# Token selection in two groups, moved into the sequence stage and into the attention

## What is computed

```python
# layer 1: recurrent mixing of the sequence
xk, xv, xr = (x * mix + shifted(x) * (1 - mix) for each of k, v, r)
k, v, r = xk @ Wk.T, xv @ Wv.T, xr @ Wr.T
per step: out = (a + exp(u + k) * v) / (b + exp(u + k)); a = a * ew + exp(k) * v; b = b * ew + exp(k)
x = layernorm(x + (sigmoid(r) * out) @ Wo.T)
# layer 2: a transformer block on 63 of the 512 tokens of each sequence
weights = x @ router_w + router_b
thr = the 64th largest weight; sel_idx = places of the 63 largest, sorted
q, k, v = rope(rmsnorm(x_sel) @ wq), rope(rmsnorm(x_sel) @ wk), rmsnorm(x_sel) @ wv     # 16 heads
x1 = x_sel + softmax(q k^T / 4 + mask[sel_idx, sel_idx]) v @ wo
x2 = x1 + gelu(rmsnorm(x1) @ w1) @ w2
x = layernorm(scatter(x2 * weight) + x * (weight <= thr))
```

## Time and profile before

| | us |
|---|---|
| median of 3 runs | 900.95 (900.33 to 901.28) |
| the profiled execution, its own time | 907.34 |
| its span, first to last instruction | 905.6 |

### The profile page before, as it was taken

The page is one execution under the profiler, slowest core; times in us unless marked ns, Lnnn a source line. Parts: engine busy times, 40 slices in busy tenths (PEclk is TensorE's granted clock), DMA queues, the critical chain, the costliest instruction groups (busy, mean ns, idle before and its releaser), DMA issues. The chain is left out here.

```text
span 905.6 us, 12959 instructions
## 1 busy us (share of the span) xinstructions
PE 779.3 (86%) x4228; PEld 522.4 (58%) x4228; DVE 729.3 (81%) x1505; ACT 496.5 (55%) x825; POOL 437.3 (48%) x303
## 2 busy tenths in 40 slices
PE   7999999999999999999999607397788888799983
PEld 4455554545555554545455405395566666699983
DVE  4689999999999999999999788446777787347773
ACT  2566757676676767676676421063567676431210
POOL 1667686868677786868686505444100000001223
PEclk9999999999999999999999855598999999999996
DMA  7122222231322223221310122342000000000000
GB/s 203 35 82 82 93 82 93 73 100 58 96 78 81 93 81 93 81 93 59 103 58 29 42 70 58 105 117 93 1 2 1 0 1 2 2 1 13 23 24 35
DMA packets 37317, 55.14 MB, mean 61 GB/s; under 512 B 3360, under 2 KB 26528, under 8 KB 37280
## 3 DMA queue, kind: packets, MB, share of 16 engines
q1 hardware_dynamic: 34464, 46.28, 16.4%
q0 software_dynamic: 2816, 8.39, 3.1%
HBM read 35.78 MB, written 18.87 MB: 60 GB/s over the span
## 5 line engine op out<-in xcount | busy, mean ns | idle before, releaser
L623 PE MATMUL ps<-arena,wa 128*128 128x512 f32 x768 | 337.0, 595 | 6.0 <-DMA wa<-w_attn 4.3
L623 PEld LDWEIGHTS ps<-arena,wa 128*128 128x128 f32 x768 | 146.2, 191 | 178.4 <-issue 169.0
L547 POOL TENSOR_TENSOR arena<-arena 128x1024 f32<-128x1024 f32 x32 | 75.5, 2360 | 123.5 <-issue 70.2
L637 PE MATMUL ps<-wa,arena 128*128 128x256 f32 x512 | 133.3, 383 | 0.0
L531 POOL TENSOR_TENSOR arena<-arena 128x512 f32<-128x512 f32 x93 | 128.1, 1407 | 4.6 <-ACT arena L915 4.6
L599 POOL TENSOR_TENSOR fst<-fst,mhalf 128x2 f32<-128x2 f32 x8 | 5.8, 720 | 235.8 <-DVE fst L1448 235.8
L928 ACT ACTIVATE arena<-arena 128x256 f32<-128x256 f32 x128 | 66.3, 590 | 67.8 <-DVE arena L1183 67.8
L1129 DVE TENSOR_TENSOR_SCAN arena<-ewb,ps 128x511 f32<-128x511 f32 x64 | 74.5, 1205 | 27.6 <-ACT ps L886 27.5
L637 PEld LDWEIGHTS ps<-wa,arena 128*128 128x128 f32 x512 | 88.4, 193 | 6.8
L538 POOL TENSOR_TENSOR arena<-arena 128x1024 f32<-128x1024 f32 x32 | 75.1, 2348 | 7.1 <-ACT arena L902 7.1
L635 PE MATMUL ps<-ident,arena 128*128 128x128 f32 x256 | 51.0, 281 | 27.3 <-POOL arena L547 27.3
(11 more groups left out here) (179 smaller groups left out, 1431.7 us busy)
## 6 DMA issues: line engine op xcount, KB each, us to landing
arena<-x_chan SPq DMA_DIRECT2D x32, 512.0 KB, 3.5
out<-arena SPq DMA_DIRECT2D x32, 512.0 KB, 3.3
arena<-x_chan SPq DMA_DIRECT2D x64, 127.8 KB, 3.2
wa<-w_attn SPq DMA_DIRECT2D x1, 1024.0 KB, 7.9
arena<-w_up SPq DMA_DIRECT2D x1, 1024.0 KB, 4.8
arena<-w_down SPq DMA_DIRECT2D x1, 1024.0 KB, 5.6
wqk<-w_qk SPq DMA_DIRECT2D x1, 512.0 KB, 4.6
wv<-w_v SPq DMA_DIRECT2D x1, 256.0 KB, 5.3
```

Source lines behind the costliest of these rows:

```text
L547: g.tensor_tensor(gg[s.par][:, :, :], num[s.par][:, :, :], ld[s.par][:, :, :], ALU.mult).then_inc(g_ready, 1)
L623: last = mm(bank[:, o, :], wa[:, m, c, o * P:(o + 1) * P], rhs, start=(c == 0), stop=(c == CC - 1))
L637: last = mm(psY[:, j, :], gg[s.par][:, c, tokens], wa[:, 3, c, :], start=False, stop=(c == CC - 1))
```

## The change

The 32 sequences are selected in two groups: group A is the first 18 (pairs 0 to 8, `SA` = 18, `NA` = 9), group B the other 14.

- Group A's selection runs in the sequence stage. VectorE has a slice of it in each of periods 21 to 30, between the numerator and the statistics; the rounds have MAX8 and MATCH_REPLACE8 but no FIND_INDEX8. A token's slot is found by counting: a scan over the tokens that are above the 63rd value or tie with it (`slots_chosen`). TensorE turns the weights in period 22 and the slots in period 27, and picks values in 28 to 30, in a bank of the key or gate projections.
- Group B's selection runs in periods 0 to 7 of the attention, before and after the softmax (`selection_early`, `selection_late`).
- Values, token index, sine and cosine are all picked by the one-hot matmul (`picks`); the tables of sine and cosine are made once at the start of the launch. The root mean square of a token comes from the statistics.
- The masks are gathered, turned, copied and picked pair by pair inside the attention: four transposes and four accumulated matmuls more on TensorE in each period, a copy on VectorE (`mask_copy`), two small copies on ScalarE (`mask_keep`).
- GpSimd gathers rows and masks through the attention and takes over the scaling of the inputs, and the last additions of the rotation (`rope_end`). It clears the value tiles in period 31. The softmax's sums stay in PSUM. The weights of the MLP are split in eight pieces in periods 11 to 17, with ScalarE.
- In the sequence stage ScalarE's order is new: the reciprocal of n-1 stands ahead of the exponentials of n, `rows_of` is one sequence later and stands ahead of the gate's logarithm. The gate's exponential is written to PSUM, and the clamp reads it there. VectorE does the statistics of n-2 ahead of the shift of n-3. The loop covers periods 4 to 19, and all else, with the attention and the MLP, is written out.

The diff, cut to what the prediction speaks of:

```diff
...
+            def gather_rows(q, batch):
...
+                g.indirect_dma_start(xsel(q), None, out_rows[0:SA * T, :] if q < NA else out_rows,
+                                     bass.IndirectOffsetOnAxis(ap=row_i[:, q:q + 1], axis=0)).then_inc(rows_in[q % 8], 16)
...
+            def rope_end(q):
...
+                for half, op in ((0, ALU.subtract), (1, ALU.add)):
+                    last = g.tensor_tensor(dst[:, :, half, :], dst[:, :, half, :], tmp[:, :, half, :], op)
+                last.then_inc(rope_done, 1)
...
+            def value_tiles_cleared():
...
+                for k in range(RING):
+                    g.memset(vblk[k], 0.0).then_inc(zeros_made, 1)
+                pool.wait_ge(zeros_made, RING)
+                pool.wait_ge(which_half, 1)
...
                 if at.exists():
                     log_sum_of(at)
+                if not isinstance(at.n, int):
+                    return
+                if at.n == 29:
+                    for q in range(0, 3):
+                        gather_rows(q, 1)
+                if at.n == 30:
+                    gather_rows(3, 2)
+                if at.n == 31:
+                    value_tiles_cleared()
             periods(pool, period)
+            last_periods(period, past=B + 1)
+            pool.wait_ge(y_ready, B)
...
+            last_periods(period, B + 1, B + 2)
+            gather_mask(0)
+            gather_mask(1)
+            normed(1)
...
+            for q in range(NP + 4):
+                if 4 <= q:
+                    normed2(q - 4)
+                if q < NP:
+                    rope_end(q)
+                if q + 2 < NP:
+                    normed(q + 2)
+                    x_of(q + 2)
+                if q + 5 < NA:
+                    gather_rows(q + 5, 2 if q == 0 else 3)
+                if q == 6:
+                    for late in range(NA, NA + 3):
+                        gather_rows(late, 4)
+                if q == 7:
+                    for late in range(NA + 3, NP):
+                        gather_rows(late, 5)
+                if q + 3 < NP:
+                    gather_mask(q + 3)
...
+                for m, bank, ready, used in ((0, psK, k_ready, den_done), (1, psV, v_ready, num_done), (2, psR, r_ready, clamp_done)):
                     if s.had(1):
                         pe.wait_ge(used, s.n)
...
+            def picks(first, past, bank, col):
...
+                for n in range(first, past):
+                    at_v = col + (PICK + 32 * tables_of(first)) * (n - first)
+                    for j in range(TJ):
+                        last = mm(ps[:, bank, at_v:at_v + 16], oh[:, n, j, :], tok_halves[:, 2 * n:2 * n + 2, j, :], start=(j == 0), stop=(j == TJ - 1))
+                    for h in range(tables_of(first)):
+                        at_t, table = at_v + 16 + 32 * h, min(2 * n + h, MB - 1)
+                        for j in range(TJ):
+                            last = mm(ps[:, bank, at_t:at_t + 32], oh[:, n, j, :], trig_halves[:, table * TJ + j, :], start=(j == 0), stop=(j == TJ - 1))
+                last.then_inc(values_picked, 1)
...
+                if n == 22 or 27 <= n <= 30:
+                    pe.wait_ge(clamp_done, n + 1)
+                if n == 22:
+                    weights_turn(0, SA, False)
+                if n == 27:
+                    slots_turn(0, SA, 5, 0)
+                if 28 <= n <= 30:
+                    picks(3 * (n - 28), 3 * (n - 28) + 3, 4, 0)
...
+            def att_period(n):
+                at = pair(n)
+                if n + 1 < NP:
+                    hn_turn(pair(n + 1))
+                    mask_turn(pair(n + 1))
+                if n < NP:
                     project_qk(at)
-                if at.is_pair(2):
...
-                    scores(at.back(1))
-                if at.below(NP):
-                    qk_turn(at, at.n + 2 if at.back(-1).below(NP) else NP)
-                if at.is_pair(4):
-                    hn2_turn(at.back(4), at.n + 1 if at.below(NP) else NP)
...
-                if s.had(2):
-                    act.wait_ge(sum_done, s.n - 1)
-                a.activation(er[s.par][:, :, :], psR[:, :, :], ACT.Exp, scale=-1.0).then_inc(er_done, 1)
+                a.activation(psR[:, :, :], psR[:, :, :], ACT.Exp, scale=-1.0).then_inc(er_done, 1)
...
+                    reciprocal_of(at.back(1))
                 if at.exists():
                     exp_k_of(at)
-                if at.had(1) and at.back(1).exists():
-                    reciprocal_of(at.back(1))
                 if at.back(-1).exists():
                     differences_scaled(at.back(-1))
                 if at.exists():
                     exp_r_of(at)
                     ln_den_of(at)
+                if at.had(4) and at.back(4).exists():
+                    rows_of(at.back(4))
+                if at.exists():
                     ln_gate_of(at)
                 if at.had(1) and at.back(1).exists():
                     evacuation_of(at.back(1))
-                if at.had(3) and at.back(3).exists():
-                    rows_of(at.back(3))
...
+            def mask_keep(at):
+                act.wait_ge(mask_picked, at.n + 1)
+                for b in range(2):
+                    block = slice(b * K, (b + 1) * K)
+                    last = a.activation(mall[block, at.n, :], ps[block, 7, 384 + b * K:384 + (b + 1) * K], ACT.Copy)
+                last.then_inc(mall_done, 1)
...
-                v.tensor_scalar(er[s.par][:, :, :], er[s.par][:, :, :], 2.0 ** 62, None, ALU.min).then_inc(clamp_done, 1)
+                if s.had(2):
+                    dve.wait_ge(sum_done, s.n - 1)
+                v.tensor_scalar(er[s.par][:, :, :], psR[:, :, :], 2.0 ** 62, None, ALU.min).then_inc(clamp_done, 1)
...
+                if isinstance(at.n, int):
+                    selection(at.n)
+                if at.had(2) and at.back(2).exists():
+                    statistics_of(at.back(2))
                 if at.had(3) and at.back(3).exists():
                     shift_of(at.back(3))
-                if at.had(2) and at.back(2).exists():
-                    statistics_of(at.back(2))
...
+            def top_round(ns, n):
+                eight = slice(8 * n, 8 * n + 8)
+                before = wsrc if n == 0 else wseq[(n - 1) % 2]
+                link(v.max(topv[0:ns, eight], before[0:ns, :]))
+                if n < K // 8 - 1:
+                    link(v.match_replace(wseq[n % 2][0:ns, :], topv[0:ns, eight], before[0:ns, :], NEG))
...
+                rows = slice(0, ns)
+                last, one = topv[rows, KC - 1:KC], ones[rows, :].to_broadcast([ns, T])
+                e, c = wseq[0][rows, :], wseq[1][rows, :]
+                if part == 0:
+                    v.tensor_copy(thr_rows[rows, :], topv[rows, K - 1:K].to_broadcast([ns, K]))
+                    v.tensor_scalar(e, wsrc[rows, :], last, None, ALU.is_equal)
+                    link(v.tensor_scalar(ties[rows, 0:KC], topv[rows, 0:KC], last, None, ALU.is_equal))
+                    v.tensor_tensor_scan(c, one, e, 0.0, ALU.mult, ALU.add)
+                    link(v.reduce_sum(need[rows, :], ties[rows, 0:KC], AX.X))
+                    link(v.scalar_tensor_tensor(e, c, need[rows, 0:1], e, ALU.is_le, ALU.mult))
+                else:
+                    link(v.scalar_tensor_tensor(e, wsrc[rows, :], last, e, ALU.is_gt, ALU.add))
+                    link(v.tensor_tensor_scan(c, one, e, 0.0, ALU.mult, ALU.add))
+                    v.tensor_tensor(e, e, c, ALU.mult).then_inc(slots_ready, 1)
...
+            def one_hot(q):
+                b = 2 * (q if q < NA else q - NA)
+                v.tensor_tensor(oh[:, q, :, :].rearrange("p j (h k) -> p j h k", h=2),
+                                slot_of[:, :, b:b + 2].unsqueeze(3).to_broadcast([P, TJ, 2, K]),
+                                slot_no[:, :].unsqueeze(1).unsqueeze(1).to_broadcast([P, TJ, 2, K]), ALU.is_equal).then_inc(oh_made, 1)
...
+            def selection(n):
+                if n == 21:
+                    token_weights(0, SA)
...
+                    top_round(SA, 0)
+                if n == 23:
+                    token_halves(0, SA)
+                    top_round(SA, 1)
+                if n == 24:
+                    top_round(SA, 2)
+                    top_round(SA, 3)
+                if n == 25:
+                    top_round(SA, 4)
+                    top_round(SA, 5)
+                if n == 26:
+                    top_round(SA, 6)
+                    top_round(SA, 7)
+                    slots_chosen(SA, 0)
+                    slots_chosen(SA, 1)
+                if n == 27:
+                    slots_copied_of(SA, 5, 0)
+                if 28 <= n <= 30:
+                    keep_values(3 * (n - 28), 3 * (n - 28) + 3, 4, 0, n - 27)
+                if 27 <= n <= 29:
+                    for q in range(3 * (n - 27), 3 * (n - 27) + 3):
+                        one_hot(q)
...
```

(31 more changed lines are left out.)

817 lines of the change are left out of this document (445 added, 372 removed).

## The result

The changed kernel takes 952.22 us (median of 4 runs, 949.78 to 956.17) against 900.64 (4 runs on the same chip): a ratio of 1.058, with a 95% interval of 1.053 to 1.063. The forecast was 881. The profiled execution has 954.52 us, span 952.8; the kernel before had 907.34, span 905.6.

The account below looks back on a forecast made before the run. It took TensorE and VectorE as both tight in the sequence stage, and a selection chain as the stretch to attack: 907.34 - 82.6 + 0.7 + 10 + 27 + 25 = 887.4, less 6.4 gives 881; range 832 to 914.

Parts of the forecast that it names:

- The loop of the sequence stage: Sequence-stage periods 2 to 25: period 16.0 instead of 15.58, plus 10 us, bounds minus 17 and plus 29.
- start: Start of the launch: one more DMA ahead of the first inputs, angle tables hidden beside the wait for inputs; plus 0.7 us.
- Rival one: Sequence stage: the gate's new place makes VectorE the bound through GpSimd; period 16.8, 915 us in all; chance 0.24.
- Rival two: Sequence stage: the sums slip through and TensorE sets the loop at 14.86; 835 us in all; chance 0.22.
- Group A's selection: Selection work placed in the sequence stage's late periods: plus 27 us, bounds 17 and 42.
- The gap: From last numerator to the attention's first projection: 107.6 us shrinks to 25 (20 to 35), minus 82.6.
- The attention: Fifteen attention periods at 10.55 plus 11 for group B, 169 against 144.7: plus 25 us, bounds 7 and 43.
- Rival three: Attention: GpSimd's queue delays it; period 11.6 instead of 10.55, 897 us, up to 915 with late gathers; chance 0.12.
- The tail: The drain and the 114 us of MLP keep their instructions: zero change.
- the distance between two scans: Sign in the sequence loop: 16.0 for the forecast, 14.9 for rival two, 16.8 for rival one.
- the sums above 1: Sign in the sequence loop: router sums averaging above 1 us would show rival one, 0.41 rival two.
- The dip of a few us in the clock: Sign between the stages: TensorE's clock at the upper level, or a dip of a few us.

Follow-up runs that it names:

- e3: Kernel before the change, with ScalarE taking the reciprocal ahead of the two exponentials of k: 898.63 us, ratio 0.982 to the kernel before.
- e8: Kernel before, with ScalarE's reciprocal ahead of the exponentials and its output rows between the two logarithms, four periods late: 926.86 us, ratio 1.028.
- e5: Changed kernel, with VectorE's shift again ahead of the statistics and ScalarE's output rows at the period's end, reciprocal still early: 876.98 us, ratio 0.971 to the kernel before.
- e6: Changed kernel, orders kept, each router sum a plain row sum with one SBUF input instead of two (other tokens chosen): 887.89 us, ratio 0.985 to the kernel before.
- e1: Changed kernel, with ScalarE again taking the reciprocal behind the two exponentials of k: 900.0 us, ratio 0.985 to the kernel before.
- e9: From e5, the two closing additions of the rotation moved from GpSimd back to VectorE: 884.64 us, ratio 0.970 to the kernel before.
- e11: From e5, group B's angle tables picked with one matmul in place of four a pair (angles wrong): 878.75 us, ratio 0.964 to the kernel before.
- e2: Changed kernel, with VectorE again taking the shift ahead of the statistics: 943.5 us, ratio 1.032 to the kernel before.
- e4: Changed kernel, with VectorE's statistics moved from the period's end to just behind the denominators: 920.49 us, ratio 1.008 to the kernel before.

## Why the prediction was wrong, step by step

**The loop of the sequence stage: the step that failed.** The forecast's parts were: VectorE's own work 13.0, waits of 3.0 taken with 3.8 as the upper bound, a period of 16.0. Own work measures 17.86 less 4.9, 13.0 exactly. The waits measure 4.9, outside the bound. It had the difference (0.6; 0.65 measured), the gate (2.35; 2.16) and one mix for the shift (0.9; 1.08), and left out the variance step, L1178 of before, which goes SBUF to SBUF like the clamp whose long time it had read, and which now stands against the first mix: 1.00. The taken value then leaned to a middle although for each kind of step in it a row spoke for the full price. And it was charged on 24 periods; the longer period lasts through the stage, in the ten selection periods too. The first 21 periods measure 41.6 more and the ten behind them 22 without the selection, 64 in place of the 10.7 for start and loop: 53 of the 57 us, and the selection is the rest.

**The cause given for it was half of it.** The prediction said that the reciprocal's new place moves the gate onto the sums. e3 shows that this move alone shortens the period, to 15.05. It needs the move of the rows as well (e8: 16.55), which the prediction doesn't mention: it costed ScalarE's reciprocal and passed over the other entry of the same queue that had moved. "GpSimd's work is moved" was argued from the exponentials behind the reciprocal; what decided was the 2.08 us of rows ahead of it.

One row of the prediction was misread: the clamp of 0.69 at 503.53 doesn't have GpSimd idle beside it but the power L554, which runs from 502.12 to 504.26. So even before, a row said that not every GpSimd instruction holds VectorE up.

**Rival one** had the mechanism and VectorE as the bound, and was priced at 915 with the same 16.8. With 2.28 more in thirty periods, 68 in place of its 29, its sum would have been 954. That this is near the 952 is partly luck: its 42 for the selection is 11 more than measured, and makes up for what gap, attention and tail cost beyond their terms. Rival two's TensorE-bound period of 14.86 exists as well: e5, e6 and e1's first part have 14.6 to 14.7. The Trainium skill, "SBUF — State Buffer", section "SBUF: two separate sides", was named for it, and by its rule the sum was this rival's; in the loop the trace agrees with the rule, down to the whole instruction being waited out (the second sum, begun 0.05 behind a gate of 2.35, ends 0.28 behind it), and the forecast should have followed it.

**Group A's selection: 27, measured 31.** Right within its bounds, though not by its terms. Periods 21 to 25 were held nearly free; in e5, where VectorE isn't bound by the waits, each of these five takes 17.4 to 18.2 against 14.7, 15 in all. In the kernel after they cost 5; that the work displaces some of the waits is a reading, not tested. The upper clock that the picks were priced at wasn't held (0.81 from 504 to 593). And of the 26.0 of the period that begins with scan 29, 7.4 are one wait that no term has. The prediction put the three row gathers at 4 or nothing. Behind them a sum waits not for one GpSimd instruction but for five:

```profile
563.66 0.94 POOL L565 DMA_INDIRECT kept<-out,row_i  x1 [0.30 <-issue]
564.37 7.78 DVE L1369 CUSTOM_DVE_ANT_0 arena<-arena,rwb 128x256 f32<-128x256 f32 x1
564.62 1.28 POOL L526 TENSOR_TENSOR arena<-arena 128x512 f32<-128x512 f32 x1
565.84 2.37 POOL L548 TENSOR_TENSOR arena<-arena 128x1024 f32<-128x1024 f32 x1
568.15 3.71 POOL L532 TENSOR_TENSOR arena<-arena 128x512 f32<-128x512 f32 x3
```

**The gap: 25, measured 28.3** from the end of the last numerators, 603.8, to 632.08. The order of events is as listed. The extra lies in three places. The gate starts 4.2 behind the numerators, where 3 were put for the clearing. The last outputs take 6.1 (610.40 to 616.5) for 4.4, at a granted clock of 0.75, and the mask's pick 2.04 for 1.06, at 0.50. The power gives 1 back: it ends 5.5 behind the statistics, not 6.5. TensorE also waits for the first mask rows (timeline), but that wait doesn't set the end: the copy of the turned mask (L1539) stands in VectorE's queue behind the last shift, which waits for GpSimd's power until 626.43.

```profile
623.83 1.12 PE L811 MATMUL ps<-ident,arena 128*128 128x128 f32 x4 [5.77 <-DMA arena<-mask_rows,msk_i]
...
626.43 0.17 DVE L1381 SCALAR_TENSOR_TENSOR arena<-arena 128x4 f32<-128x4 f32 x1 [5.39 <-POOL arena L555]
...
628.14 0.68 DVE L1539 COPY arena<-ps 128x512 f32<-128x512 f32 x1
628.96 2.04 PE L821 MATMUL ps<-halves,arena 128*128 128x128 f32 x8 [4.01 <-DVE arena L1539]
```

**The attention: 25, measured 28.6, by two errors that cancel.** The steady period is 9.91, not 10.55: the new wait for GpSimd's additions, put at 0.7, is worth 0.08 (e9). Group B costs 173.1 less fifteen times 9.91, 24.4, not 11: the prediction charged VectorE's 28 us and forgot that its 56 picks stand in TensorE's queue, and that TensorE's clock would fall there (0.77 from 674 to 726), which e11 shows to be most of the price of periods 5 and 6. The 24 stood in the text only as an upper bound. Rival three's late gathers were not seen: the pairs behind the eighth go at 9.9.

**The tail: 0, measured 1.9.** Its cause is open.

What the profile was to show came out so: the distance between two scans beyond 16.8, the sums above 1 in the steady stage (1.10 on average from 100 to 330), about 25 in the gap, 9.9 for 10.5. "Wrong it would be by a loop outside 14.9 to 16.8" is what happened. The dip of a few us in the clock was more than that (0.68 on average over the 29 us of the gap), and TensorE did wait for a gather, the first masks' (5.77), though that didn't set the end of the gap.

## What to carry to other kernels

Where VectorE and GpSimd are both used, list for each VectorE step whether its operands are all in SBUF, and lay it against GpSimd's instructions of the period; price each meeting at what is left of the GpSimd instruction, up to the whole of it, small steps included (the exceptions seen are below). When a queue is reordered, follow what stood ahead of each moved entry as well as what stood behind it: here moving two entries of ScalarE's queue, which carries neither engine's work, was worth 2.8% in one direction and, with the right one of them alone, 1.8% in the other. And a busy share of 99% is not work: compare the mean of each group with its shortest instance.

## What the runs showed of the hardware

With both queues full the engines took turns instruction by instruction in e1: a waiting VectorE step goes when the GpSimd instruction ends, and the next GpSimd instruction goes before the next VectorE step (1.41 a turn). This isn't a rule for all cases. In the kernel after one sum waits through five GpSimd instructions in a row (7.78 at 564.37, shown above), and so it is in e2 (7.66, five) and e6 (a variance step, 5.85, four). All three stand right behind the row gathers; what denies VectorE its turn there is open. GpSimd waits too: the gate takes 2.56 for 2.35 when it meets a sum (e8), the mixes 4.27 for 3.74 (e1).

Which VectorE steps wait, as far as these traces show: two SBUF inputs (the sums; the shift on 128x4, 0.15 to 2.35; the one-hot products on 128x512, 0.68 to 2.83), `tensor_scalar` from SBUF to SBUF (128x4, 0.17 to 5.85; 128x1024, 0.69 to 1.82) and the copy of the statistics from SBUF to SBUF (128x28, 0.16 to 1.31). Not: any with an input in PSUM (in all fourteen traces), the statistics L1362, the plain sums of e6, or the selection's replacement (0.66, wholly beside the gate in e1).

Which GpSimd steps are waited for: the products, sums, mixes and scalings on 256 and more elements a partition. Not the power on 128x8, though it takes 1.65 to 1.85: in e4, 85 sums start beside it and none takes over 0.43.

```profile
316.02 1.85 POOL L555 TENSOR_TENSOR arena<-arena,mhalf 128x8 f32<-128x8 f32 x1
316.29 0.42 DVE L1370 CUSTOM_DVE_ANT_0 arena<-arena,rwb 128x256 f32<-128x256 f32 x1
```

And the sums don't wait for a clearing. In the kernel after, beside GpSimd's four memsets, they take their 0.42:

```profile
605.30 2.03 POOL L608 MEMSET arena<- 128x544 f32 x4
...
605.92 0.42 DVE L1369 CUSTOM_DVE_ANT_0 arena<-arena,rwb 128x256 f32<-128x256 f32 x1
```

The same section of the Trainium skill says that two SBUF inputs are blocked only against a GpSimd step that reads SBUF; these rows agree. The power reads SBUF too and blocks no sum; there the rule says more than is measured, and the measurement decides.
